# When the first attention vectors are loaded, and where the edge one-hots and counts stand, in a four-layer GNN and FFN kernel

## The reference

```python
def gat_layer(x, W, a_s, a_d, b, edge_index, concat):
    n = x.shape[0]
    H, C = a_s.shape
    h = (x @ W).reshape(n, H, C)
    src, dst = (edge_index[0], edge_index[1])
    alpha_s = jnp.einsum('nhc,hc->nh', h, a_s)
    alpha_d = jnp.einsum('nhc,hc->nh', h, a_d)
    e = jax.nn.leaky_relu(alpha_s[src] + alpha_d[dst], NEG_SLOPE)
    m = jax.ops.segment_max(e, dst, num_segments=n)
    e = jnp.exp(e - m[dst])
    denom = jax.ops.segment_sum(e, dst, num_segments=n)
    alpha = e / (denom[dst] + EPS)
    msg = h[src] * alpha[:, :, None]
    out = jax.ops.segment_sum(msg, dst, num_segments=n)
    ...
```

## Time and profile before

| what | value |
|---|---|
| executions | 1412.08, 1413.95, 1419.55 us |
| median | 1413.95 us |
| span of the profiled execution | 1413.3 us |
| what lies around the span, against the median | 0.65 us |
| PE busy | 1359.0 us (96%) |
| DVE busy | 1070.8 us (76%) |
| ACT busy | 852.4 us (60%) |
| DMA, mean over the span | 314 GB/s |

### The profile page before, as it was taken

The page is one execution under the profiler, slowest core; times in us unless marked ns, Lnnn a source line. Parts: engine busy times, 40 slices in busy tenths (PEclk is TensorE's granted clock), DMA queues, the critical chain, the costliest instruction groups (busy, mean ns, idle before and its releaser), DMA issues.

```text
span 1413.3 us, 17174 instructions
## 1 busy us (share of the span) xinstructions
PE 1359.0 (96%) x6806; PEld 1100.3 (78%) x6806; DVE 1070.8 (76%) x932; ACT 852.4 (60%) x604; POOL 21.5 (2%) x47
## 2 busy tenths in 40 slices
PE   6999999889999999999899999999999999999998
PEld 4676776568888888888655788888888888888887
DVE  7877532558888888886442788888888888888886
ACT  5666231336777777773223577777777777777774
POOL 2000100000000000000000000000000000000000
PEclk9999999999999999999999999999999999999999
DMA  9987643468999899994165879998998999989980
GB/s 380 414 321 290 265 170 147 158 252 342 381 363 362 359 382 363 359 385 182 60 253 201 339 311 376 366 362 360 379 366 357 364 383 358 363 360 383 362 355 12
DMA packets 42256, 443.23 MB, mean 314 GB/s; under 512 B 4736, under 2 KB 4768, under 8 KB 7408
## 3 DMA queue, kind: packets, MB, share of 16 engines
q1 hardware_dynamic: 39312, 427.05, 75.2%
q0 software_dynamic: 2912, 15.74, 3.0%
HBM read 442.38 MB, written 0.39 MB: 313 GB/s over the span
## 4 chain that ended last, share of the span: by engine, by line
PE 85%; DVE 7%; issue 4%; ACT 2%; DMA 1%; POOL 0%; SPq 0%; POOLq 0%; DVEq 0%; ACTq 0%
PE AC L1385 22%; PE PJ L1364 14%; PE PJ L1366 14%; PE PJ L1365 14%; PE AC L1247 2%; PE TP L1373 2%; PE AC L1235 2%; PE PJ L1151 2%; DVE w_lo_g L888 1%; DMA ring<-in_weights 1%; PE MS L1128 1%; PE PJ L1161 1%; PE PJ L1163 1%; PE PJ L1162 1%; PE PJ L1208 1%
## 5 line engine op out<-in xcount | busy, mean ns | idle before, releaser
L888 DVE TENSOR_TENSOR w_lo_g<-ring,w_hi_g 128x3072 fp32r<-128x3072 f32 x54 | 181.3, 3358 | 59.1 <-ACT w_hi_g L578 59.0
L888 DVE TENSOR_TENSOR w_lo_d<-ring,w_hi_d 128x3072 fp32r<-128x3072 f32 x50 | 167.9, 3358 | 26.5 <-ACT w_hi_d L578 26.5
L1364 PE MATMUL PJ<-w_hi_u,XTl 128*128 128x512 f32 x450 | 182.5, 405 | 0.0
L1364 PE MATMUL PJ<-w_hi_g,XTl 128*128 128x512 f32 x450 | 176.7, 393 | 4.8 <-DVE w_lo_g L888 4.7
L578 ACT ACTIVATE w_hi_d<-ring 128x3072 fp32r<-128x3072 f32 x50 | 139.5, 2790 | 69.1 <-PE AC L1385 69.1
L1366 PE MATMUL PJ<-w_hi_g,XTh 128*128 128x512 f32 x450 | 176.0, 391 | 0.0
L1366 PE MATMUL PJ<-w_hi_u,XTh 128*128 128x512 f32 x450 | 175.9, 391 | 0.0
L1365 PE MATMUL PJ<-w_lo_g,XTh 128*128 128x512 f32 x450 | 175.8, 391 | 0.0
L1365 PE MATMUL PJ<-w_lo_u,XTh 128*128 128x512 f32 x450 | 175.2, 389 | 0.0
L888 DVE TENSOR_TENSOR w_lo_u<-ring,w_hi_u 128x3072 fp32r<-128x3072 f32 x52 | 174.3, 3352 | 1.0 <-ACT w_hi_u L578 1.0
L578 ACT ACTIVATE w_hi_u<-ring 128x3072 fp32r<-128x3072 f32 x52 | 145.1, 2791 | 39.0 <-PE PJ L1366 39.0
(11 more groups left out here) (295 smaller groups left out, 2116.4 us busy)
## 6 DMA issues: line engine op xcount, KB each, us to landing
ring<-in_weights SPq DMA_DIRECT2D x202, 1536.0 KB, 9.3
extra<-in_weights SPq DMA_DIRECT2D x69, 1536.0 KB, 9.5
extra<-in_attn POOLq DMA_DIRECT2D x12, 768.0 KB, 9.5
extra<-in_attn POOLq DMA_DIRECT2D x6, 512.0 KB, 6.7
scratch<-in_ffn_vectors POOLq DMA_DIRECT2D x1, 2688.5 KB, 12.3
extra<-in_x SPq DMA_DIRECT2D x1, 384.0 KB, 3.4
out<-extra SPq DMA_DIRECT2D x1, 384.0 KB, 2.3
rows<-in_rows POOLq DMA_DIRECT2D x1, 192.0 KB, 14.9
```

Of the source, the lines that this page charges most:

```text
L888: v.tensor_tensor(wl[dst or kind][:], slab_at(n), wh[dst or kind][:].bitcast(F32), ALU.subtract).then_inc(S("lo_" + kind), 1)
L1364: mm(dst, XTl[:, t, :], wh[kind][:, w], start=(t == 0), stop=False)
```

## The change

The loads of vector units 0 and 1 move from the head of POOL's instructions to behind the first layer norm's power, and POOL waits there until slab 1 has landed. The loads of rows, cols and small stand behind them as before. The one-hots move on DVE from behind lo(s1) to behind lo(s3), and the counts on PE from behind project(1) to behind project(2).

```diff
-            vectors(0)
-            vectors(1)
             nc.gpsimd.memset(power[:], -0.5).then_inc(S("const_filled"), 1)
...
             ln_power(0)
+            landed(pool, 1)
+            vectors(0)
+            vectors(1)
             pool.dma_start(rows[:], rows_in).then_inc(S("small_loaded"), 16)
...
                         split_lo(w1_slab(c, 3 * g + 1))
-                    if g == 0:
-                        edges_one_hot()
-                    elif g < groups:
+                    if 0 < g < groups:
                         logits(c, g - 1)
...
                     if g == 0:
                         wide_terms(0)
                         split_lo(w1_slab(c, 3))
+                        edges_one_hot()
...
                             project(c, per * g + j)
-                            if g == 0 and j == 1:
+                            if g == 0 and j == per - 1:
                                 edge_counts()
```

## The result

The changed kernel takes 1418.57 us in the median of 20 executions (1416.45 to 1420.36), the kernel before 1414.01 us in 20 (1409.31 to 1419.55): 4.56 us more, a ratio of 1.0032 with a 95% interval of 1.0021 to 1.0042. In the means it is 1418.52 against 1414.40, 4.1 us more. Forecast were 1418.0 us and a loss of 4.1.

The account below looks back on a forecast made before the run. PE was taken to set the time. Its wait for the one-hots and the slower clock after it put slab 5 at 46.4 against 42.27, +4.1 us; 1413.3 + 4.1 + 0.65 gave 1418.0 us, range 1412.5 to 1421.5.

Parts of the forecast that it names:

- What bounds the kernel: Whole span: PE is 85% of the chain of waits; a delay PE takes in the first 25 us is not made up.
- The loads: First loads: slab 1 lands 2.7 us sooner, at 11.5; gain at most 1.4 us on DVE; units land at 22.3 and 28.0.
- rival 3: At terms(0): vector unit 0 lands at 27.5, DVE and PE stand 3.4 us more; +7.5, 1421.5 us; chance 0.06.
- rival 2: At slab 2: it lands no sooner than 20.99, all from there 1.65 us later; +5.8, 1419.7 us; chance 0.10.
- DVE's order: DVE before slab 2's low part: a gap of 1.37 us goes, one of 3.05 comes; net +1.7 us, hidden.
- PE's wait: PE before the counts: stands 7.5 us for the one-hots, ready at 34.25, with slab 3 behind the counts.
- The clock: PE after its wait: runs at its lower level for 3.39 us, costing 1.7 us; bounds 0 and 3.4.
- Rival 1: PE after its wait: the clock stays up, slab 5 starts at 44.7; +2.4, 1416.4 us; chance 0.15.
- Rival 4: Further back: idle gaps and clock phases drawn anew; losing both dips, worth 5.1 us, gives -1.0, 1412.9 us; chance 0.10.
- Rival 5: Whole chain: shortened by DVE's 1.4 us to 1412.5 us, needing one-hots done by about 30; chance 0.03.

Follow-up runs that it names:

- ACT's order: Changed kernel with ACT's high part of slab 2 taken ahead of copy(0): mean 2.2 us above the kernel before, ratio 1.0022.
- late loads alone: Kernel before with only POOL's part of the change, one-hots and counts in their old places: mean 1.3 us below the kernel before, ratio 0.9994.
- 30 dummies: Changed kernel with 30 dummy matmuls of 128 columns on PE ahead of the counts: mean 1.2 us above the kernel before, ratio 1.0009.
- with 60: Changed kernel with 60 dummy matmuls of 128 columns on PE ahead of the counts: mean 8.3 us above the kernel before, ratio 1.0061.
- the counts behind slab 3: Changed kernel with PE's counts moved one slab further back, behind project(3): mean 2.4 us above the kernel before, ratio 1.0015.
- the one-hots early: Changed kernel with DVE's one-hots back behind slab 1's low part, counts in the new place: mean 1.5 us below the kernel before, ratio 0.9989.
- the new order only: Kernel before with only the DVE and PE parts of the change, vector units loaded first: mean 4.4 us above the kernel before, ratio 1.0025.

## Why the prediction was right

**What bounds the kernel.** Right: PE's delay in the first 50 us went to the end, less or more by what the clock did later.

**The loads.** Slab 1 was ready for ACT at 12.08 (12.3 forecast), with no wait, and DVE's gap of 1.37 went. The vectors landed as worked out: 10.0 and 15.1 us after their issues near 12.0 and 12.5, that is at 22.0 and 27.6 (22.3 and 28.0):

```profile
DMA to landing us min/median/max: 10.0/12.5/15.1
```

terms(0) did not wait; rival 3 did not come about, and neither did rival 2: ACT took slab 2 at 19.15 without a wait for it, and in the run with ACT's order it was there by 17. The gain that I gave the loads, 1.4 us on DVE, is what the late loads alone have: 1.7 in the place of slab 5, 1.3 in the mean time.

**DVE's order.** The hole of 3.06 us (3.05 forecast), released by ACT, and slab 4's low part at 37.52 (37.55). That they meet to the hundredth is luck, for the end of PE's slab 0 moves with the length of its slow start: the same hole was 2.91, 3.54 and 4.40 us in the profiles with 30 dummies, with 60 and with the counts behind slab 3. The experiment with ACT's order shows that the hole hangs on ACT's order and not on the stream, as argued.

**PE's wait.** 7.31 us (7.5), counts at 34.23 (34.4), slab 3 behind them, though DVE had begun its low part at 26.00. That this, and not DVE's 1.64, sets the loss stands in the changed kernel's own rows: DVE starts slab 4's low part at 37.52, and PE comes to slab 4 only at 42.75 and waits for nothing. With the counts behind slab 3 it is the other way round: slab 4 waits for DVE, and 1.86 us of the loss are gone. With the one-hots early both go, and all of the loss with them; that run does not part the two.

**The clock.** The step was right and its size too small. I took 1.7 us; the counts and slab 3 lost 2.64. The lower level held from the counts on to 39.87, 5.6 us in place of the 3.39 of the earlier trace rows; the cost is inside my bounds of 0 and 3.4. A part was offset: between the term rows' first row and slab 4 there were 0.81 us, where I had 1.05 with PE's running out. Both together, with counts that start 0.17 sooner than forecast, make 46.95 in place of 46.4: 4.68 us late, not 4.1. That the means differ by 4.1 us, the forecast to the tenth, is luck: the loss in place was 0.6 larger, and the standard error of the difference is 0.66. Rival 1, a clock that stays up, is what the 30 dummies made: 44.02 where it said 44.7.

**Rival 4,** gaps further back drawn anew, happened in part: 1.23 us came back at 241 us in the two profiled executions. It does not show in the medians. The 20 executions of the changed kernel fall into two groups, six with spans of 1414.6 to 1415.4 us at a mean clock of 0.995 and fourteen of 1416.3 to 1418.4 at 0.992 to 0.993. So the same instructions meet the lower level for a different time from execution to execution, and the one profile of a kernel is a draw of that. The Trainium skill, "TensorE: Matmul & The Clock Gate", Part 1, says that one kernel shows different numbers of slow matmuls from run to run; these groups agree with it. The mean clock of the changed kernel was 0.9930, that of the kernel before 0.9950 to 0.9958 in three comparisons: 2.8 to 4.0 us of 1413, though a part of it falls into PE's idle time, where it costs nothing.

**Rival 5,** a shorter chain as a whole, is what the loads give without the new order; my reason against it, that the one-hots can't be done by 30 behind lo(s3), held.

## What to carry to other kernels

Before an instruction is moved into a new place, look at what the gap in its old place was for: here a DVE instruction that filled a wait of 3 us was moved to where it filled none, and the wait stayed. When a producer moves back, every consumer on an in-order engine blocks all that stands behind it, here a slab that had been ready for 6 us; moving the consumer back as far as its result allows takes part of the loss away. And a wait on PE has two prices, its own length and the slow matmuls after it, of which the second was here the larger (2.64 of 4.68 us); cheap dummy matmuls that fill the wait and don't outlast it show which is which.

## What the runs showed of the hardware

After 7.3 us of idle time the lower clock held for 5.6 us of work, beginning with 16 small bf16 matmuls (34.23 to 39.87). In the run with the new order only, after 7.35 us of idle time and the same small matmuls, it held from 37.19 to 41.08, 3.9 us; in the run with ACT's order, after 6.83 us, from 34.68 to 38.91, 4.2 us. In the kernel before it held for 3.4 us, without such a gap. From the counts to the term rows the three took 7.71, 6.86 and 6.98 us where 5.07 is the time at the full clock, so nearly the same wait cost 2.64, 1.79 and 1.91 us. The clock had fallen during the wait: over it the granted clock was 0.68 on the mean in the changed kernel (27.0 to 34.23 us) and 0.80 in the run with the new order only (29.8 to 37.19).

A vector load of 768 KB on POOL's queue delays the weight slab beside it just as much when it is issued 4 us later (slab 1 taken at 14.07 against 14.28, and 15.59 in another run with the early issue). Of the issues tried, only the one behind slab 1's landing kept it clear.

A comparison of 128x2048 elements, with both inputs broadcast (the row of numbers over the tiles, the edge list over the columns), took DVE 2.25 us, with 32-bit and with 16-bit operands alike.

Late loads with early one-hots were the fastest of all, 1.0 to 1.5 us below the kernel before in the three kernels that have them. Each interval alone holds no change, so that it beats the kernel before is likely and not shown.
